# First expert's values in split products: who makes the remainders

## The reference, cut to what matters

```python
base1 = t @ w1.T; base3 = t @ w3.T
h1 = base1[None] + SCALING * einsum('etr,efr->etf', einsum('td,erd->etr', t, a1), b1)
h3 = base3[None] + SCALING * einsum('etr,efr->etf', einsum('td,erd->etr', t, a3), b3)
act = silu(h1) * h3
out_e = einsum('etf,df->etd', act, w2) + SCALING * einsum('etr,edr->etd', einsum('etf,erf->etr', act, a2), b2)
out = einsum('te,etd->td', weights, out_e)
```

## Time and profile before

| | |
|---|---|
| median of 3 runs | 968.78 us (968.59 to 969.45) |
| the profiled execution | 970.89 us, of which the span from first to last instruction is 969.1 us |
| mean granted clock of TensorE | 0.989 of full speed |
| busy: PE, DVE, POOL, ACT | 919.5, 685.0, 592.3, 555.7 us |
| first layer | about the first 630 us; slots 1 and 2 take some 30.5 us each, slots 6 to 10 some 41 |

### The profile page before, as it was taken

How to read it: one execution, slowest core, us unless ns; L and a number is a source line. 1 busy time by engine, 2 the same in 40 slices (tenths; PEclk the granted TensorE clock), 3 DMA queues, 4 the chain that set the end, 5 groups by cost and what they waited for, 6 DMA issues and landing times. The chain is left out here.

```text
span 969.1 us, 17609 instructions
## 1 busy us (share of the span) xinstructions
PE 919.5 (95%) x5060; PEld 698.9 (72%) x5067; DVE 685.0 (71%) x2098; ACT 555.7 (57%) x1255; POOL 592.3 (61%) x565
## 2 busy tenths in 40 slices
PE   6999999999999999999999999889998999989996
PEld 3777777777777767777767776568994676658996
DVE  5657678888888797888898787474542567665553
ACT  4444655766757577674664443135663676635663
POOL 5678868868577586776867876544441244552443
PEclk8899999999999999999999999999999999999999
DMA  6890000000000000000000000435544000005552
GB/s 182 356 404 2 1 1 1 1 1 1 1 1 1 1 1 1 2 0 1 12 1 12 13 1 27 146 105 179 180 148 119 2 13 23 24 32 152 179 178 87
DMA packets 39774, 62.74 MB, mean 65 GB/s; under 512 B 7073, under 2 KB 23266, under 8 KB 37504
## 3 DMA queue, kind: packets, MB, share of 16 engines
q1 hardware_dynamic: 35136, 53.08, 16.7%
q0 software_dynamic: 4544, 8.54, 2.6%
HBM read 34.68 MB, written 27.82 MB: 64 GB/s over the span
## 5 line engine op out<-in xcount | busy, mean ns | idle before, releaser
L384 PE MATMUL bank<-split 128*128 128x512 f32 x544 | 244.0, 448 | 5.8 <-POOL split L1816 3.0
L386 PE MATMUL bank<-split 128*128 128x512 f32 x544 | 214.9, 395 | 0.0
L385 PE MATMUL bank<-split 128*128 128x512 f32 x544 | 213.8, 393 | 0.0
L909 ACT ACTIVATE sil<-bank 128x512 f32<-128x512 f32 x128 | 76.0, 594 | 147.2 <-PE bank L386 146.7
L384 PEld LDWEIGHTS bank<-split 128*128 128x128 f32 x544 | 103.0, 189 | 36.0 <-issue 10.4
L385 PEld LDWEIGHTS bank<-split 128*128 128x128 f32 x544 | 103.4, 190 | 26.3 <-issue 10.5
L1295 DVE TENSOR_TENSOR act<-bank,sil 128x512 f32<-128x512 f32 x128 | 87.7, 685 | 48.3 <-PE bank L386 25.4
L386 PEld LDWEIGHTS bank<-split 128*128 128x128 f32 x544 | 102.9, 189 | 23.8
L1772 POOL TENSOR_TENSOR act<-act 128x512 f32<-128x512 f32 x64 | 88.6, 1384 | 27.9 <-DVE act L1301 27.7
L1778 POOL TENSOR_TENSOR split<-act,split 128x512 fp32r<-128x512 f32 x64 | 89.7, 1403 | 16.5 <-ACT split L976 16.2
L735 PE MATMUL bank<-xlT,e 128*128 128x128 f32 x624 | 84.2, 278 | 7.8 <-ACT hT_e L1172 4.5
(11 more groups left out here) (314 smaller groups left out, 2010.7 us busy)
## 6 DMA issues: line engine op xcount, KB each, us to landing
e<-e_dram SPq DMA_DIRECT2D x78, 256.0 KB
rows_in<-yw SPq DMA_DIRECT2D x17, 1056.0 KB, 17.9
xin<-rows_in SPq DMA_DIRECT2D x78, 66.0 KB
e<-e_dram SPq DMA_DIRECT2D x4, 512.0 KB, 7.9
x<-rows_out SPq DMA_DIRECT2D x8, 256.0 KB, 4.6
rows_in<-yw,slot_i POOLq DMA_INDIRECT x64, 2.3
rows_out<-ob,ids POOLq DMA_INDIRECT x39
out<-ob,ids POOLq DMA_INDIRECT x39
```

Source lines behind the costliest of these rows:

```text
L384: mm(dst, w[0], m[0], start=start, stop=False, **more)
L385: mm(dst, w[0], m[1], start=False, stop=False, **more)
L386: return mm(dst, w[1], m[0], start=False, stop=stop, **more)
L909: af(sil[(k - 1) % 2][:, :], bank[BH1[STEPS[k - 1][0] % 2]][:, :], ACT.Silu).then_inc(silu_done.sem, 1)
```

## The change: what it does, and the diff

First values become split products. ACT rounds each `act0[j]` to fp32r (`first_high_of`), a remainder is taken (`first_low_of`), and `value` runs three fp32r matmuls for each block in place of one f32 product, with the split a2 that value_sum used already; it now waits for the remainders. Of the four remainders of a slot, blocks 0 and 1 go to POOL in attention slots and to DVE elsewhere; blocks 2 and 3 always go to DVE. ua and ud get a second buffer each, buffers are laid out anew in SBUF, and some semaphores are merged (two of the tokens' statistics, the tanh step, and the products and bias parts at the end of the first layer, where DVE's bias parts now start after ACT's four copies).

```diff
-            ua, ud = [sb(f"ua{k}", [P, S]) ...], [sb(f"ud{k}", [P, S]) ...]
+            ua, ud = ([[masked_u[:, (4 * p + 2 * k + i) * S:(4 * p + 2 * k + i + 1) * S] for i in range(2)] for p in range(2)] for k in range(2))
+            firsts = [(part(47 + j), part((5, 6, 51, 52)[j])) for j in range(J)]
# PE, value(js)
+                        if g == 0:
+                            pe.wait_ge(weight_rest.sem, len(LOW_POOL) + 2)
                     for j in js:
-                        pe.wait_ge(*act_done(g, STEP[j, 0]))
-                        last = mm(bank[BV][:, :], a2[:, j, :], act0[j][:, :], start=j == 0, stop=j == J - 1)
+                        pe.wait_ge(*(first_low(g, j + 1) if j < 2 else last_low(g, j - 1)))
+                        last = mm3(bank[BV][:, :], tuple(w[:, rows(j)] for w in a2s), firsts[j], j == 0, j == J - 1)
# ACT
+                def first_high_of(j):
+                    if g is None:
+                        return
+                    act.wait_ge(*act_done(g, STEP[j, 0]))
+                    act.wait_ge(*v_ready(g - 1, 1))
+                    af(firsts[j][0], act0[j][:, :], ACT.Copy).then_inc(first_high.sem, 1)
                 a_high()
+                first_high_of(0)
+                first_high_of(1)
                 silu(3)
...
                 mask(1)
+                first_high_of(2)
                 silu(6)
...
                 a_mid(1)
+                first_high_of(3)
                 a_gate(1)
# DVE
+                def first_low_of(j):
+                    if g is None or j < 2 and s.a_up is not None:
+                        return
+                    dve.wait_ge(*first_high(g, j + 1))
+                    if j < 2:
+                        dve.wait_ge(*summed(g, j + 1))
+                    v.tensor_tensor(firsts[j][1], act0[j][:, :], firsts[j][0].bitcast(F32), ALU.subtract
+                                    ).then_inc((first_low if j < 2 else last_low).sem, 1)
# DVE, masked(i)
-                    dve.wait_ge(*u_low(q - 1))
+                    dve.wait_ge(*h3_ready(q - 2))
                 a_leaky(0)
+                first_low_of(0)
+                first_low_of(1)
+                first_low_of(2)
                 masked(0)
+                first_low_of(3)
                 act(7)
# POOL
+                def first_low_of(j):
+                    if g is None or s.a_up is None:
+                        return
+                    pool.wait_ge(*first_high(g, j + 1))
+                    pool.tensor_tensor(out=firsts[j][1], in0=act0[j][:, :], in1=firsts[j][0].bitcast(F32), op=ALU.subtract
+                                       ).then_inc(first_low.sem, 1)
                 total(1)
+                first_low_of(0)
                 sums_low(g, 0)
...
                 r_scale(s.r_stat)
+                first_low_of(1)
                 up_low(q, 0, 0)
# DVE, end of the first layer
             tables(0)
+            dve.wait_ge(late_made.sem, 4)
             bias_parts()
-            dve.wait_ge(prod_saved.sem, 4)
```

## The result

The changed kernel took 982.74 us, median of 6 runs (979.2 to 985.74), where the kernel before took 968.74 in the same rounds: ratio 1.0129, 95% interval 1.0113 to 1.0145. The profiled execution took 982.14 with a span of 979.5, so 11.25 more than the profiled one of before and a span 10.4 longer. The medians differ by 14.0. Of that the traces can explain only the 10.4: the profiled execution of before was 2.15 slower than its median, that of the changed kernel 0.6 faster than its own, and the remaining 0.85 lies around the spans. The direction was forecast; the size, 3.15, was not, and the time lies outside the range, 964 to 979.

A forecast was written before the change was run, and what follows sets the result against it. PE (TensorE, 95% busy) was taken to bound the kernel. Losses and gains, 3.5 - 4.7 + 2.75 + 1.6, made 3.15 us lost on the median 968.78: 972.0 forecast, own range 969.1 to 975.9, with rivals 964 to 979.

The forecast's parts named there:

- the size, 3.15: The sum of all terms over the kernel: 3.15 us lost.
- The saving and the added work: First values on PE 2.76 for 3.43, saving 0.67 a slot; remainders 0.60 each on DVE; ACT copies and layout at nothing.
- The multiply at 361.72: DVE weighting multiply that ran its 0.69 inside a POOL power operation; taken as evidence that such operations do not block remainders.
- Where the remainders stand: Three DVE remainders ahead of masked(0) in slots 0 to 4 and 13 to 15 make it 1.80 late; up(1) waits behind.
- Slots 0 to 4: Saved 3.35, waits at up(1) 6.88; net 3.5 us lost.
- is not repaid later: Slots 0 to 4: the wait at up(1) stays lost, since PE's work between two slots is back to back.
- Slots 5 to 12: Attention slots: saving counts in seven of eight, net gain 4.7 us, bounds 5.4 and 2.7.
- slot 9: PE already waits 0.53 for DVE's z there, so the 0.67 of slot 8 is lost in a longer wait.
- Slots 13 and 14: Loss 2.75 us, 1.75 and 1.0, about the middle between POOL taking no part and handing all lateness on.
- POOL's chain: Slots 13 and 14: 92% busy up to lora_out, taken to hand on part of the lateness, with 1.52 us idle.
- Slot 15: Saving goes into PE's wait for POOL's sums_low; act(8) 1.56 late; loss 1.6 us, bounds 0.9 and 2.4.
- much slower: Rival: POOL's power operation blocks the remainders, 1.17 more in slots 1 to 4, 13 and 14, 7.0 in all; 979; chance 0.13.

The follow-up runs named there:

- e4: Changed kernel without the 64 remainders, the second pass taking the rounded copy again; 964.50 us, ratio 0.9946.
- e5: Changed kernel's buffers, doubled masks and merged semaphores, but the f32 products of before and no copies or remainders; 971.59 us, ratio 1.0008.
- e2: Changed kernel with only ACT's order changed: yn_f made ahead of up_high(1); 980.21 us, ratio 1.0101.
- e1: Changed kernel with only DVE's order changed: masked(0) ahead of all four remainders; 987.62 us, ratio 1.0181.
- e8: Changed kernel with remainders 0 and 1 made by POOL in slots 0 to 4 and 13 to 15 too, no longer DVE; 981.49 us, ratio 1.011.
- e3: Changed kernel with both orders changed: masked(0) ahead of the remainders on DVE, yn_f ahead of up_high(1) on ACT; 980.94 us, ratio 1.0107.
- e10: The changed kernel again with no edit, for a second trace; 982.76 us, ratio 1.0135.
- e11: As e1, but in slots without attention POOL's first up_low waits until the last remainder is done; 988.17 us, ratio 1.0189.
- e6: Changed kernel with split values only in slots 5 to 12, f32 products in the other eight; 966.96 us, ratio 0.9961.
- e7: Changed kernel; in slots without attention remainder 0 before act(5), value 1 f32, remainders 2 and 3 later; yn_f ahead of up_high(1); 969.70 us, ratio 0.9993.
- e9: Slots 5 to 12 as in the changed kernel, 0 to 4 as in e7, 13 to 15 with f32 products of before; 965.97 us, ratio 0.9951.

## Why the prediction was wrong, point by point

*The saving and the added work* were right: 2.75 for 2.76, 0.60 a remainder, copies covered, layout free (e4, e5). The multiply at 361.72, by which the rule of the Trainium skill (SBUF — State Buffer, Who interferes with whom) was put aside for POOL's power operation, judged well: the three remainders at 109.72 ran in their 0.60, two of them begun inside the one from 109.25 to 110.89, and none of the 24 remainders that began inside a power operation in the changed kernel took over 0.70.

*The step that failed* is "Where the remainders stand", applied in "Slots 0 to 4". It names up(1) as the product that waits and follows masked(1) only to POOL; that the wait "is not repaid later" was taken as the end of the account. ACT was left out. masked(1) is late by four remainders, 2.4, not three; ACT's queue carries that over up_high(1) to yn_f; and PE meets it there. A slot pays for the latest path, in slot 2 by waits of 1.61 + 0.63, not for the first. e2 took that path away alone and 3.1 us came back; e1 freed up(1) and e8 halved its wait, and what went there came back at yn_f.

*Slots 0 to 4* lost 6.38 for 3.5 by act(1). The starts of PE's gate product, one early in each slot, show slot by slot where:

| | slot 0 | 1 | 2 | 3 | 4 | 5 |
|---|---|---|---|---|---|---|
| start, before | 31.08 | 57.01 | 87.50 | 118.44 | 152.16 | 187.76 |
| start, changed | 30.27 | 56.94 | 89.37 | 122.26 | 156.50 | 193.03 |
| start, e2 | 29.47 | 55.48 | 87.12 | 119.18 | 153.29 | 189.79 |
| longer, forecast | -0.02 | +1.13 | +1.13 | +0.37 | +0.92 | |
| longer, changed | +0.74 | +1.94 | +1.95 | +0.52 | +0.93 | |
| longer, e2 | +0.08 | +1.15 | +1.12 | +0.39 | +0.90 | |

The excess stands in slots 0, 1 and 2, where PE waits for yn_f, about 0.8 each, and in no other. With yn_f out of the way (e2) each of the five slots comes out as forecast within 0.1. So this part of the sum was right but for the one path that it left out.

*Slots 5 to 12* gained 3.94 for 4.7 (3.41 by the gate products). DVE does use up the saving in places, as forecast for slot 9; slot 11 kept little either (0.04, or 0.22 by the gate products).

*Slots 13 and 14* lost 5.29 for 2.75, and this term is the other one mis-sized. Besides yn_f, PE waits 1.31 at 531.98 for DVE's residual add. Rows of that moment in the changed kernel:

```profile
530.00 1.23 DVE L1545 TENSOR_TENSOR inv<-invs,sc_r 128x4 f32<-128x4 f32 x1
531.16 0.68 DVE L1467 TENSOR_TENSOR x<-bank,x 128x512 f32<-128x512 f32 x1
...
528.69 1.30 POOL L1796 TENSOR_TENSOR act<-act 128x512 f32<-128x512 f32 x1 [2.64 <-DVE act L1312]
529.96 1.26 POOL L1809 TENSOR_TENSOR split<-act,split 128x512 fp32r<-128x512 f32 x1
```

The same two instructions in e4:

```profile
518.93 0.15 DVE L1541 TENSOR_TENSOR inv<-invs,sc_r 128x4 f32<-128x4 f32 x1
...
519.11 1.29 POOL L1805 TENSOR_TENSOR split<-act,split 128x512 fp32r<-128x512 f32 x1 [0.20 <-ACT split L976]
```

A 128x4 multiply took 1.23 beside POOL's subtraction, which had begun 0.04 before it. In e4 the multiply is first by 0.18 and takes 0.15, and PE does not wait. So it is in all thirteen traces: the multiply takes 1.23 to 1.25 and PE waits 0.96 to 1.33 in the changed kernel, e1, e2, e3, e8, e10 and e11; it takes 0.15 and PE does not wait in the other six. What decides which of the two begins first is not shown, and no run isolates this cause. POOL's chain, which was to bind, did so only once the waits ahead of it were cleared (e2, e3).

*Slot 15* and the tail lost 1.14 for 1.6, inside the bounds, with luck: up to the wait for `nxt` 2.0 are lost (the fall of the clock at 615 to 618 among them), and 0.9 come back because the clock did not fall there as it did before.

*The second layer* was taken as unchanged, and is 1.5 longer in the profile, 2.4 in e10. It was unchanged in e5, within 0.2 in e6 and 0.8 longer in e7, but 2.0 to 4.5 longer in e1 to e4, e8, e9 and e11. Layout is not the cause (e5), nor how late the first layer ends (e4 ends it first of all), nor the clock, which was at its upper level from the first expert matmul to the last 14 us in every trace. In e3 and e8 part of it are PE's waits for the transfers that load the experts' rows (2.5 in all, for 1.1 before); in the changed kernel these are 1.1 as before. The cause stays open.

*The rivals*: "much slower", 979, came nearest in time and was wrong in its mechanism; that it was near is luck.

## What to carry to other kernels

When an edit makes one engine late, follow the lateness down every queue that waits for it, to each place where the bounding engine takes delivery, and charge the latest arrival: clearing the first wait only uncovers the next. An operation with no dependence on the late data is late all the same if it stands behind one that has, so look for it in the order of the third engine. Price such a change stage by stage, and use it only in stages with cover: here the stages with cover alone turn 1.3% slower into 0.4% faster (e6). And before a slot is called worse by its waits alone, look at the granted clock in it.

## What the runs showed of the hardware

A DVE subtraction of two SBUF tiles of 128x512 takes a step of 0.60 (0.68 long); where it began inside a POOL subtraction of 128x512 it took 1.78 (e1: four took 3.59 for 2.49), and holding POOL back restored 2.49 (e11). That agrees with the Trainium skill (SBUF — State Buffer, Who interferes with whom), by which the second comer stands for the whole of the first. Beside POOL's power operations of 128x4 and 128x8 no such wait shows (24 subtractions, 0.70 at most). The price does not go with size: a 128x4 operation took 1.23 for 0.15 beside a POOL subtraction. The granted clock fell to 0.50, 1.2 GHz, for about 3 us behind an idle time of PE of 2.31 in slot 1 of e1, and stayed at 1.00 behind one of 2.33 in slot 2; where it fell, the slot took about 1.6 more. The order of waits in the first layer is repeatable to 0.1 us a slot between two executions, while the expert stage, which waits for transfers, differed by 0.9.
